# Building a graph's adjacency matrices: laps without a branch, crowded groups done afterwards, one weight product for three

## The chip, the cores and the metric

The kernel runs on one core of one Trainium2 chip. The metric is device time in microseconds for one execution, the median of three runs. The profile is of one further execution.

## The reference, cut to what matters

Four graph layers run one after the other over 3125 nodes and 103125 edges (a GCN with edge weights, a GAT with four heads, a dot-product attention, a two-step GraphSAGE), each followed by a layer norm. All four need sums over the edges that arrive at each node:

```python
msgs = edge_val[:, None] * xw[edge_col]
out = segment_sum(msgs, edge_row, num_segments=3125)      # layer 0
out = segment_sum(h[src] * alpha[:, :, None], dst, 3125)   # layer 1, softmax over each node's edges
numer = segment_sum(w[:, None] * V[sender], receiver, 3125)   # layer 2, softmax again
agg = segment_sum(x[src], dst, 3125) / max(deg, 1)         # layer 3, twice
```

The edges come sorted by destination (`dst`), on average 33 to a node.

## The kernel before, in words

Instead of gathering and scattering, the kernel builds two dense matrices in device memory (`adjacency`): for each pair (destination, source) how many edges there are and the sum of their weights. Afterwards every layer is dense matrix work over tiles of 128 nodes.

The change lies in the first two of its stages.

`edge_tables` prepares the edges. Nodes are taken in groups of three destinations (`WD = 3`), 1056 groups in all. VectorE finds by comparisons where each group's edges start in the sorted list (`start`, and `held`, which is `start` limited so that 128 entries can be read). GpSimd then fetches, for each group, the 128 edges from that place on (`own`, nine indirect DMAs, 128 groups each). TensorE transposes them in three batches (L388), ScalarE copies the transposes out of PSUM (`ids`, `weight`, L416), and VectorE unpacks each batch (the helper at L263 to L283) into the table `near`: for edge slot p of group w, a key (destination in the group times 40, plus the high part of the source), a low part of the source (0 to 79), and the weight as three bf16 parts. Groups that hold more than 128 edges need further chunks. For them the stage also makes flat tables in one partition, `before_row` (running count of extra chunks) and `first_row`, and a table `limits` that holds, in all partitions, up to which edge each group has been read. Each flat row takes nine transposes (L374) and a copy (L408), one row after the other; `limits` takes one more row, a product with a row of ones (L379), and a copy (L411). TensorE issues all of these ahead of the transposes at L388, and ScalarE ahead of the copies at L416.

`build_matrices` runs 88 laps of twelve groups. In each lap

- VectorE makes one-hot rows of the low parts (L483) and of the keys (L485), and multiplies the former by each of the three weight parts (L489, three instructions);
- TensorE multiplies keys by low parts, three matmuls for each group, 36 in a lap (L525), of which the last stands alone behind the part described next;
- ScalarE copies the 120 x 1920 results from PSUM to one of two halves of `bm_stage` (L557), after the store of that half two laps earlier has landed;
- SyncE stores the half, 900 KB (L566).

The one-hots, the four PSUM banks that a lap writes and the staging area are double: lap n uses what lap n - 2 used. VectorE and TensorE both call `beyond` in each lap: they read two entries of `before_row` into registers (L451), compare them (L456), and only if they differ go through the lap's groups with further chunks. The loop holds two laps to a round (L446). The stage ends when the last store has landed; the next stage reads what was stored.

Of the kernel before, what the change touches and what calls it, by code (L numbers as in the profile page):

```python
# [56 lines left out]
RING = 2  # L57
DST_BITS = 12
# [48 lines left out]
def edge_tables(nc, k):  # L107

    with ExitStack() as ctx:
# [3 lines left out]
        def sem(name):  # L113
# [14 lines left out]
        edge_i = sb("edge_i", [P, ECOL], I32)  # L128
# [23 lines left out]
        lim = sb("lim", [P, WT])  # L152
# [4 lines left out]
        row = sb("flat_row", [1, NWP])  # L157
# [6 lines left out]
         flat_taken, spread) = map(  # L164
            sem, ("consts", "pads", "noughts", "below_ready", "falls_ready", "counted", "rows_ready", "pair_ready",
                  "starts_ready", "cols_turned", "cols_taken", "et_turned", "et_taken", "dve_done", "start_ready",
                  "shifted", "more_ready", "et_summed", "before_ready", "flattened", "flat_taken", "et_spread"))
# [4 lines left out]
        N_CONSTS = 17  # L172
# [35 lines left out]
        def _(pool):  # L208
# [23 lines left out]
            pool.iota(edge_i[:, :], pattern=[[P, ECOL]], base=0, channel_multiplier=1).then_inc(consts, 1)  # L232
# [19 lines left out]
        def _(dve):  # L252
# [50 lines left out]
            step(dve.tensor_copy(k.edge_at[:], edge_i[:]))  # L303
# [18 lines left out]
            step(dve.tensor_scalar(lim[:], held[:], float(P), None, ALU.add))  # L322
            floor(first[:], lim[:], P)
# [3 lines left out]
            step(dve.tensor_tensor(more[:], end[:], lim[:], ALU.is_gt))  # L327
            step(dve.tensor_tensor(more[:], more[:], past[:], ALU.mult))
# [63 lines left out]
        def _(act):  # L392
# [13 lines left out]
            for n, flat_row in enumerate((k.before, k.first, row)):  # L406
# [3 lines left out]
            act.wait_ge(spread, 1)  # L410
            act.activation(k.lim[:].rearrange("p (b c) -> p b c", c=BW), ps[:, 2:2 + BATCHES, 0:BW], ACT.Copy)  # L411
# [7 lines left out]
def build_matrices(nc, k):  # L419


    with ExitStack() as ctx:
# [3 lines left out]
        def sem(name):  # L426
            return ctx.enter_context(nc.semaphore(name))

        OH = sb("bm_oh", [P, RING, LW // 2, 1 + PARTS, SL, 2], BF16)
        gate = sb("bm_gate", [P, 1])  # L430
        more_key = sb("bm_more_key", [P, P], BF16)
        more_oh = sb("bm_more_oh", [P, 1 + PARTS, SL], BF16)
        stage = sb("bm_stage", [KEYS, 2, LW, 2, SL])
        ps = ctx.enter_context(nc.psum_tensor("bm_ps", [P, 8, BANK], F32))
        used, lows, made, copied, more_step, more_made, more_used = map(
            sem, ("bm_used", "bm_lows", "bm_made", "bm_copied", "bm_more_step", "bm_more_made", "bm_more_used"))
# [5 lines left out]
        WIDE = 2 * SL  # L442

        def each_lap(eng, work):
# [8 lines left out]
        def beyond(eng, lap, work):  # L453

            most = LAPS * LW * NCH
            with eng.If(table(eng, k.before, lap * LW, most) < table(eng, k.before, lap * LW + LW, most)):  # L456
                with eng.Fori(0, BANKS) as b:
                    with eng.Fori(0, PER_BANK) as i:
                        w = eng.snap(lap * LW + b * PER_BANK + i)
                        begin = table(eng, k.before, w, most)  # L460
                        end = table(eng, k.before, w + 1, most)
                        first = table(eng, k.first, w, NCH)
                        with eng.If(begin < end):
                            with eng.Fori(begin, end) as at:
                                c = nc.s_assert_within(eng.snap((at - begin) + first), 0, ECOL - 1,
                                                       skip_runtime_bounds_check_because=WHY)
                                work(at, w, c, b, i)
                        table(eng, k.first, w, NCH)
                table(eng, k.first, lap * LW, NCH)

        @block.vector
        def _(dve):
            dve.sem_inc(more_used, 1)

            def onehots(lap, u, two):
                wide_low, wide_key = [P, LW // 2, SL, 2], [P, LW // 2, KEYS, 2]

                def spread(f, wide):
                    return (k.near[:, f, bass.ds(lap * LW, LW)].rearrange("p (a b) -> p a b", b=2).unsqueeze(2)
                            .to_broadcast(wide))  # L480

                dve.wait_ge(used, lap + 1)
                dve.tensor_tensor(OH[:, u, :, 0], k.low_grid[:].unsqueeze(1).to_broadcast(wide_low),  # L483
                                  spread(1, wide_low), ALU.is_equal).then_inc(lows, 1)
                dve.tensor_tensor(k.KEY[:, u, :, 0:KEYS], k.key_grid[:].unsqueeze(1).to_broadcast(wide_key),  # L485
                                  spread(0, wide_key), ALU.is_equal)
# [5 lines left out]
                def more(at, w, c, b, i):  # L492
                    dve.wait_ge(more_used, at + 1)
                    dve.tensor_tensor(gate[:], k.edge_at[:, bass.ds(c, 1)], k.lim[:, bass.ds(w, 1)], ALU.is_ge
                                      ).then_inc(more_step, 1)
                    dve.tensor_scalar(more_key[:], k.iota_key[:], k.key_base[:, bass.ds(w, 1)],
                                      k.col_key[:, bass.ds(c, 1)], ALU.add, ALU.is_equal).then_inc(more_step, 1)
                    dve.tensor_scalar(more_oh[:, 0], k.iota_low[:], k.col_low[:, bass.ds(c, 1)], None, ALU.is_equal
                                      ).then_inc(more_step, 1)
                    dve.wait_ge(more_step, at * 3 + 3)  # L500
                    dve.tensor_scalar(more_key[:], more_key[:], gate[:], None, ALU.mult)
                    for v in range(PARTS):
                        last = dve.tensor_scalar(more_oh[:, 1 + v], more_oh[:, 0], k.col_parts[:, v, bass.ds(c, 1)], None,
                                                 ALU.mult)
                    last.then_inc(more_made, 1)

                beyond(dve, lap, more)

            each_lap(dve, onehots)

        @block.tensor
        def _(pe):
# [3 lines left out]
            def products(lap, u, two):  # L516
                def place(i, v):
                    b, c = divmod(i, PER_BANK)
                    return ps[:, 4 * u + b, c * WIDE + SL * (v > 0):(c + 1) * WIDE]

                def body(i, planes):
# [1467 lines left out]
```

## Time and profile before

| | |
|---|---|
| time, median of 3 runs | 2430.63 us (2427.82 to 2435.46) |
| the profiled execution | 2439.62 us, of which its span 2437.9 us |
| edge tables | 0 to about 81 us |
| the 88 laps | about 81 to 443 us, the last store to about 450 us |
| busy over the whole span | PE 78%, VectorE 72%, ScalarE 46%, GpSimd 5% |

Engines are PE (TensorE's matmuls), PEld (its weight loads), DVE (VectorE), ACT (ScalarE), POOL (GpSimd) and SP (SyncE). A row of the timeline gives start, duration, engine, line, operation, what it writes and reads, its shapes and, in brackets, how long the engine was idle before it and what ended the idleness; "x35" are 35 instructions merged into a row. A q behind an engine's name is its sequencer: register loads, comparisons and branches, which do not count as busy. The shares over the whole span say little here, since the change touches only the first 450 us; all rows below are therefore of stretches in it, but for those on instruction fetches.

### The profile page before, as it was taken

To read this page: it belongs to the slowest core of one execution; us is meant where nothing else is said; L and a number is where in the kernel's file an instruction comes from. 1 tells how busy PE (TensorE), PEld (TensorE's weight loads), DVE (VectorE), ACT (ScalarE), POOL (GpSimd) and SP (SyncE) were. 2 spreads that over 40 slices of the span, in tenths; PEclk is the share of its full clock that TensorE was granted. 3 is DMA by queue.
4 is the path that set the end of the run, shared out by engine and by line. 5 is a ranking of instruction groups with operands and counts; after the bars stand their busy time and mean duration, and the time that the engine had idled before them with its cause. 6 is when DMAs were issued, how large, how long until landed. Compare 5 with 4: busy or idle time off the path is not lost. (4 is left out here: it accounts for less than half of the span.)

```text
span 2437.9 us, 44362 instructions
## 1 busy us (share of the span) xinstructions
PE 1902.0 (78%) x16121; PEld 1441.9 (59%) x16122; DVE 1753.2 (72%) x1874; ACT 1133.4 (46%) x1959; POOL 127.3 (5%) x225
## 2 busy tenths in 40 slices
PE   3456666699478888898888888873899999498794
PEld 2456555444456666676666667652688887354452
DVE  4887877100359999999999999855788885572375
ACT  1344444100257777677777777632666664101001
POOL 4000000000000000000000000000000000010120
PEclk6787877799689999999999999986899999699897
DMA  3488888999023443322444432211865650492492
GB/s 103 116 235 230 231 221 220 237 270 244 6 62 103 111 110 109 97 50 73 110 109 110 109 79 59 82 39 35 162 129 108 133 108 3 188 409 112 204 420 76
DMA packets 582353, 341.98 MB, mean 140 GB/s; under 512 B 397008, under 2 KB 574312, under 8 KB 575640
## 3 DMA queue, kind: packets, MB, share of 16 engines
q1 hardware_dynamic: 579928, 338.61, 50.4%
q0 software_dynamic: 720, 1.77, 0.3%
q10 hardware_dynamic: 1648, 0.83, 0.1%
q8 instruction: 37, 0.61, 0.1%
q14 instruction: 20, 0.16, 0.0%
HBM read 214.18 MB, written 127.01 MB: 140 GB/s over the span
## 5 line engine op out<-in xcount | busy, mean ns | idle before, releaser
L1207 ACT ACTIVATE exponentials<-gr_ps,att_cols 128x256 f32<-128x256 f32 (+1 forms) x1300 | 493.3, 491 | 185.1 <-PE gr_ps L1097 183.3
L1097 PE MATMUL gr_ps<-ident,gr_r 128*128 128x128 f32 x2500 | 381.8, 292 | 69.0 <-DVE gr_r L1315 67.0
L1097 PEld LDWEIGHTS gr_ps<-ident,gr_r 128*128 128x128 f32 x2500 | 284.1, 147 | 153.0 <-issue 130.8
L1128 PE MATMUL gr_ps<-exponentials,heads 128*33 128x128 f32 x5000 | 363.5, 277 | 14.1 <-DVE exponentials L1322 14.1
L1322 DVE SCALAR_TENSOR_TENSOR exponentials<-exponentials,gr_count_t 128x3072 f32<-128x3072 f32 (+1 forms) x104 | 349.0, 3355 | 21.9 <-ACT exponentials L1207 17.9
L1288 DVE CUSTOM_DVE_ANT_0 gr_unread<-gr_src_rows,gr_closed 128x3125 bf16<-128x3125 f32 (+1 forms) x100 | 344.2, 3442 | 17.0 <-ACT gr_closed L1200 16.6
L525 PE MATMUL bm_ps<-bm_oh,key_onehots 128*128 128x80 bf16 (+1 forms) x3168 | 228.9, 238 | 146.6 <-issue 119.4
L525 PEld LDWEIGHTS bm_ps<-bm_oh,key_onehots 128*128 128x128 bf16 x3168 | 202.7, 112 | 172.8 <-issue 169.3
L1128 PEld LDWEIGHTS gr_ps<-exponentials,heads 128*33 128x33 f32 x5000 | 254.1, 110 | 80.5 <-issue 55.9
L557 ACT ACTIVATE bm_stage<-bm_ps 120x1920 f32<-120x1920 f32 x88 | 156.0, 1773 | 220.8 <-DMA adjacency<-bm_stage 119.5
L798 PE MATMUL sage_ps<-sage_counts,sage_parts 128*128 128x400 bf16 x1200 | 207.4, 337 | 14.6 <-DVE sage_counts L832 14.6
L1315 DVE TENSOR_SCALAR gr_r<-gr_src_rows,gr_lift_u,gr_floor_u 128x3125 f32<-128x3125 f32 (+1 forms) x100 | 188.0, 1921 | 13.1 <-PE gr_ps L1097 7.5
L798 PEld LDWEIGHTS sage_ps<-sage_counts,sage_parts 128*128 128x128 bf16 x1200 | 118.6, 99 | 104.1 <-DVE sage_counts L832 16.0
L1546 PE MATMUL ar_ps<-KT,ar_left 128*128 128x400 f32 x400 | 147.1, 512 | 16.2 <-DVE ar_low_u L1637 14.7
L489 DVE TENSOR_TENSOR bm_oh<-bm_oh,near 128x960 bf16<-128x960 bf16 x264 | 157.4, 652 | 0.0
L698 PE MATMUL agg_gcn_ps<-agg_gcn_ring,agg_gcn_left 128*128 128x400 f32 x400 | 142.5, 512 | 14.3 <-DMA agg_gcn_ring<-adjacency 14.2
L1565 PEld LDWEIGHTS ar_ps<-ar_pt,X 128*128 128x128 f32 x1250 | 145.5, 192 | 11.5 <-ACT ar_pt L1609 4.5
L1565 PE MATMUL ar_ps<-ar_pt,X 128*128 128x128 f32 x1250 | 147.8, 275 | 0.0
L832 DVE CAST sage_counts<-sage_ring 128x3200 bf16<-128x3200 f32 x50 | 93.7, 1874 | 47.6 <-POOL sage_ring L788 47.6
L710 DVE COPY agg<-agg_gcn_ps 128x1600 f32<-128x1600 f32 x1 | 1.8, 1825 | 173.4 <-PE agg_gcn_ps L698 173.4
L698 PEld LDWEIGHTS agg_gcn_ps<-agg_gcn_ring,agg_gcn_left 128*128 128x128 f32 x400 | 75.6, 193 | 81.3 <-issue 30.6
L1609 ACT ACTIVATE ar_pt<-ar_ps 128x512 f32<-128x512 f32 (+1 forms) x175 | 84.0, 547 | 77.4 <-PE ar_ps L1555 77.4
(319 smaller groups left out, 1970.2 us busy)
## 6 DMA issues: line engine op xcount, KB each, us to landing
sage_ring<-count_by_source SPq DMA_DIRECT2D x50, 1600.0 KB, 9.3
adjacency<-bm_stage SPq DMA_DIRECT2D x88, 900.0 KB, 5.8
agg_gcn_ring<-adjacency SPq DMA_DIRECT2D x25, 1600.0 KB, 14.4
gr_count<-adjacency SPq DMA_DIRECT2D x25, 1600.0 KB, 9.3
ar_counts<-adjacency SPq DMA_DIRECT2D x25, 1600.0 KB, 9.1
count_by_source<-gr_count_t SPq DMA_DIRECT2D x12, 3200.0 KB, 16.7
fg_node<-gat_node_sums SPq DMA_DIRECT2D x1, 1650.0 KB, 6.3
count_by_source<-gr_count_t SPq DMA_DIRECT2D x1, 1600.0 KB, 7.1
```

What stands on the lines that cost most here:

```text
L489: last = dve.tensor_tensor(OH[:, u, :, 1 + v], OH[:, u, :, 0], spread(2 + v, wide_low), ALU.mult)
L525: last = pe.matmul(place(i, v), k.KEY[:, u, a, :, b], moving, start=i % PER_BANK == 0 and v == 0, stop=True, skip_group_check=True)
L557: act.activation(stage[:, u].rearrange("p (b w) v c -> p b (w v c)", b=BANKS), ps[0:KEYS, BANKS * u:BANKS * (u + 1), 0:PER_BANK * WIDE], A ...
L698: last = pe.matmul(ps[:, b, 0:CW], left[:, u, :], ring[:, u, b * CW:(b + 1) * CW], start=False, stop=True, skip_group_check=True)
L798: last = pe.matmul(ps[:, b, 0:CW], parts[:, u, i, :], counts[:, u, b * CW:(b + 1) * CW], start=False, stop=True, skip_group_check=True)
L1097: last = pe.transpose(ps[:, i % RINGS, c:c + P], r[:, j, s * P:(s + 1) * P], k.ident[:])
L1128: last = pe.matmul(ps[j * PAIR:j * PAIR + C + 1, 7, 0:P], heads[:, h, s, :], e[:, s, j * P:(j + 1) * P], start=s == 0, stop=s == NT - 1, s ...
L1207: last = act.activation(e[:, s, 0:w], ps[:, i % RINGS, c:c + w], ACT.Exp, bias=cols[:, h, s:s + 1])
L1288: dve.tensor_tensor_reduce(out=unread[:, 0:n], in0=src_rows[:, h, 0:n], in1=closed[:, j, 0:n], scale=1.0, scalar=FLOOR, op0=ALU.subtract, ...
L1315: last = dve.tensor_scalar(r[:, j, 0:n], src_rows[:, h, 0:n], lift_u[:, h, j:j + 1], floor_u[:, h, j:j + 1], ALU.add, ALU.max)
L1322: dve.scalar_tensor_tensor(part, part, 1.0, count_t[:, first:last, 0:w], ALU.min, ALU.mult).then_inc(weighed, 1)
L1565: last = pe.matmul(ps[:, 7, 0:P], k.X[:, first + j, :], pt[:, i, j * P:(j + 1) * P], start=first + j == 0, stop=first + j == NT - 1, skip_ ...
```

## The change

- **Laps.** `beyond` is gone from the laps: neither VectorE nor TensorE reads a table or branches inside one. The 36 matmuls of a lap stand together.
- **Crowded groups.** Behind the last lap, `each_crowded` goes down from all groups to 96, to twelve, to one, wherever the running count differs, and rebuilds a group of more than 128 edges whole: VectorE makes one-hots for each chunk, TensorE accumulates, ScalarE copies out and stores over the group's place. ScalarE begins this only once all stores of the laps have landed.
- **Tables.** `first` now counts from the group's own start, and a group counts as crowded by `end - start > 128`. `limits`, `edge_at` and the flat row that fed `limits` are gone, with nine transposes, six matmul instructions and two ScalarE copies.
- **Products.** The weights' one-hots of a lap come from one VectorE instruction over 2880 elements in each partition, where there were three over 960. For that the parts are the outer dimension of `bm_oh`, and `near` is laid out lap by lap, so the unpacking writes runs of twelve elements.
- **Loop.** Four laps make a round instead of two.

```diff
+UNROLL = 4
 # edge_tables
-            step(dve.tensor_copy(k.edge_at[:], edge_i[:]))
-            step(dve.tensor_scalar(lim[:], held[:], float(P), None, ALU.add))
-            floor(first[:], lim[:], P)
+            floor(first[:], start[:], P)
+            step(dve.tensor_tensor(crowd[:], end[:], start[:], ALU.subtract))
-            step(dve.tensor_tensor(more[:], end[:], lim[:], ALU.is_gt))
-            step(dve.tensor_tensor(more[:], more[:], past[:], ALU.mult))
+            step(dve.scalar_tensor_tensor(more[:], crowd[:], float(P), past[:], ALU.is_gt, ALU.mult))
-                unpack(ids[:, cols], weight[:, cols], BW, k.near[:, 0, cols], k.near[:, 1, cols],
-                       [k.near[:, 2 + v, cols] for v in range(PARTS)], k.key_base[:, cols])
+                mine = [k.near[:, b * (BW // LW):(b + 1) * (BW // LW), f, :] for f in range(2 + PARTS)]
+                unpack(ids[:, cols], weight[:, cols], BW, mine[0], mine[1], mine[2:], k.key_base[:, cols])
-            for n, column in enumerate((before, first, lim)):
+            for n, column in enumerate((before, first)):
-            pe.wait_ge(flat_taken, 3)
-            for b in range(BATCHES):
-                last = pe.matmul(ps[:, 2 + b, 0:BW], ones[0:1, :], row[:, b * BW:(b + 1) * BW], start=True, stop=True)
-            last.then_inc(spread, 1)
-            for n, flat_row in enumerate((k.before, k.first, row)):
+            for n, flat_row in enumerate((k.before, k.first)):
-            act.wait_ge(spread, 1)
-            act.activation(k.lim[:].rearrange("p (b c) -> p b c", c=BW), ps[:, 2:2 + BATCHES, 0:BW], ACT.Copy)
 # build_matrices
-            with eng.Fori(0, LAPS // 2) as two:
-                for u in range(2):
-                    work(two * 2 + u, u, two)
+            with eng.Fori(0, LAPS // UNROLL) as some:
+                for u in range(UNROLL):
+                    work(some * UNROLL + u, u % 2, some * (UNROLL // 2) + u // 2)
+        def each_crowded(eng, work):
+            def inside(w, sizes):
+                begin = table(eng, k.before, w, MOST)
+                end = table(eng, k.before, w + sizes[0], MOST)
+                with eng.If(begin < end):
+                    if len(sizes) == 1:
+                        work(w, begin, end)
+                    else:
+                        with eng.Fori(0, sizes[0] // sizes[1]) as i:
+                            inside(eng.snap(i * sizes[1] + w), sizes[1:])
+                    table(eng, k.first, w, NCH)
+            inside(0, (LAPS * LW, 96, LW, 1))
 # VectorE, one lap
-                for v in range(PARTS):
-                    last = dve.tensor_tensor(OH[:, u, :, 1 + v], OH[:, u, :, 0], spread(2 + v, wide_low), ALU.mult)
-                last.then_inc(made, 1)
-                beyond(dve, lap, more)
+                low = OH[:, u, 0].rearrange("p a c b -> p (a c b)").unsqueeze(1)
+                dve.tensor_tensor(OH[:, u, 1:].rearrange("p v a c b -> p (v a) c b"), low.to_broadcast([P, PARTS, LW * SL]),
+                                  near(2, PARTS).to_broadcast([P, PARTS * (LW // 2), SL, 2]), ALU.mult).then_inc(made, 1)
 # TensorE, one lap
-                for i in range(LW - 1):
-                    body(i, range(PARTS))
-                body(LW - 1, range(PARTS - 1))
-                beyond(pe, lap, more)
-                body(LW - 1, range(PARTS - 1, PARTS)).then_inc(used, 1)
+                for i in range(LW):
+                    a, b = divmod(i, 2)
+                    for v in range(PARTS):
+                        moving = OH[:, u, 0:2, a, :, b] if v == 0 else OH[:, u, 1 + v, a, :, b]
+                        last = pe.matmul(place(i, v), k.KEY[:, u, a, :, b], moving, start=i % PER_BANK == 0 and v == 0,
+                                         stop=True, skip_group_check=True)
+                last.then_inc(used, 1)
             each_lap(pe, products)
+            pe.wait_ge(copied, LAPS + 2)
+            each_crowded(pe, redo)
 # ScalarE
             each_lap(act, copy_out)
+            for s in range(2):
+                act.wait_ge(stored[s], 16 * (LAPS // 2) + 16)
+            each_crowded(act, redo)
```

## Rows read from the trace of the kernel before

**Rows 1.** Busy time of each engine over the laps, with granted clock, DMA share, GB/s.
```profile
82.00:443.00 361.00, 228.88 (x3168) 202.73 (x3168) 279.02 (x439) 155.98 (x88) 0.00 (x0) 0.81 0.81 221
```

**Rows 2.** Waits in the laps: total us, times, longest us.
```profile
ACT bm_stage L557 <- DMA adjacency<-bm_stage: 119.5, 54, 3.2
ACT bm_stage L557 <- PE bm_ps L525: 101.3, 34, 22.4
```

**Rows 3.** The timeline of ScalarE's copies, one to a lap.
```profile
88.54 1.77 ACT L557 ACTIVATE bm_stage<-bm_ps 120x1920 f32<-120x1920 f32 x1 [22.37 <-PE bm_ps L525]
96.51 1.77 ACT L557 ACTIVATE bm_stage<-bm_ps 120x1920 f32<-120x1920 f32 x1 [3.11 <-DMA adjacency<-bm_stage]
...
239.19 1.77 ACT L557 ACTIVATE bm_stage<-bm_ps 120x1920 f32<-120x1920 f32 x1 [1.90 <-DMA adjacency<-bm_stage]
...
246.56 1.77 ACT L557 ACTIVATE bm_stage<-bm_ps 120x1920 f32<-120x1920 f32 x1 [1.53 <-DMA adjacency<-bm_stage]
...
389.05 1.77 ACT L557 ACTIVATE bm_stage<-bm_ps 120x1920 f32<-120x1920 f32 x1 [2.93 <-DMA adjacency<-bm_stage]
...
441.15 1.77 ACT L557 ACTIVATE bm_stage<-bm_ps 120x1920 f32<-120x1920 f32 x1 [1.03 <-PE bm_ps L525]
```

**Rows 4.** The stores of the laps (L566), from issue to landing.
```profile
DMA to landing us min/median/max: 5.4/5.8/7.0
```

**Rows 5.** Instructions of TensorE and VectorE in the laps, by line.
```profile
L525 PE MATMUL bm_ps<-bm_oh,key_onehots 128*128 128x80 bf16 (+1 forms) x3168 | 228.9, 238 | 146.6 <-issue 119.4 <-DVE bm_oh L489 26.5
...
L489 DVE TENSOR_TENSOR bm_oh<-bm_oh,near 128x960 bf16<-128x960 bf16 x264 | 157.4, 652 | 0.0
...
L485 DVE TENSOR_TENSOR key_onehots<-key_grid,near 128x1440 bf16<-128x1440 int16 x88 | 79.3, 902 | 0.0
L483 DVE TENSOR_TENSOR bm_oh<-low_grid,near 128x960 bf16<-128x960 int16 x87 | 57.3, 658 | 75.7 <-PE bm_ps L525 74.0 <-issue 1.4
```

**Rows 6.** The timeline of TensorE: 35 matmuls of a lap, at either clock.
```profile
243.01 1.88 PE L525 MATMUL bm_ps<-bm_oh,key_onehots 128*128 128x160 bf16 x35 [0.39 <-issue]
...
433.73 3.29 PE L525 MATMUL bm_ps<-bm_oh,key_onehots 128*128 128x160 bf16 x35 [0.40 <-issue]
```

**Rows 7.** Table reads and branch (lines L451, L456): ns min/median/max.
```profile
L451 PEldq TENSOR_LOAD <-before_row x176: 298/624/1487, 86.2 to 440.0; - x176
...
L456 PEldq COMPARE_BRANCH  x88: 212/212/253, 87.9 to 440.6; - x88
```

**Rows 8.** The timeline from the last load of edges to the end of unpacking.
```profile
45.44 0.95 POOL L244 DMA_INDIRECT own<-edge_pairs,held_i  x1 [0.30 <-issue]
...
52.45 1.12 ACT L408 ACTIVATE first_row<-ps_tab 1x1152 int32<-1x1152 f32 x1 [2.17 <-PE ps_tab L374]
53.62 1.58 PEld L374 LDWEIGHTS ps_tab<-ident,lim 128*1 128x1 f32 x9 [1.71 <-ACT first_row L408]
...
61.04 1.56 PE L388 MATMUL ps_tab<-ident,own 128*128 128x128 f32 x6
...
63.16 0.36 DVE L271 TENSOR_SCALAR scratch_i<-ids 128x384 int32<-128x384 int32 x1 [16.22 <-ACT weight L416]
...
79.75 0.56 DVE L283 TENSOR_TENSOR near<-scratch,near 128x384 bf16<-128x384 f32 x1
```

**Rows 9.** DMA issues up to 100 us: the indirect loads of edges, us to landing.
```profile
own<-edge_pairs,held_i POOLq DMA_INDIRECT x9, 2.8
```

**Rows 10.** The timeline of VectorE: one unpaired product at two sizes.
```profile
28.16 1.09 DVE L281 TENSOR_TENSOR scratch<-col_weight,col_parts_b 128x896 f32<-128x896 f32 x1
...
67.31 0.56 DVE L281 TENSOR_TENSOR scratch<-weight,near 128x384 f32<-128x384 f32 x1
```

**Rows 11.** One round of the GAT stage's loop (L1020): busy time, instruction counts.
```profile
924.50:996.10 71.60, 61.82 (x664) 49.01 (x660) 70.32 (x41) 51.60 (x115) 3.35 (x2) 0.98 0.34 93
```

**Rows 12.** DMA queues over the whole span: packets, MB, share of 16 engines.
```profile
q8 instruction: 37, 0.61, 0.1%
```

**Rows 13.** DMA queues from 1000 to 1500 us; it is the only queue listed.
```profile
q1 hardware_dynamic: 98448, 46.82, 34.5%
```

More of the change, by code:

```diff
@@ L442, in build_matrices @@
         WIDE = 2 * SL
+        MOST = LAPS * LW * NCH
         def each_lap(eng, work):
-            with eng.Fori(0, LAPS // 2) as two:
-                for u in range(2):
-                    work(two * 2 + u, u, two)
+            with eng.Fori(0, LAPS // UNROLL) as some:
+                for u in range(UNROLL):
+                    work(some * UNROLL + u, u % 2, some * (UNROLL // 2) + u // 2)
         def table(eng, t, w, most):
             return eng.value_load(t[0:1, bass.ds(w, 1)], min_val=0, max_val=most)
[L453 to L469, printed above, removed]
@@ L471, in _, with onehots, near @@
         @block.vector
         def _(dve):
-            dve.sem_inc(more_used, 1)
-            def onehots(lap, u, two):
+            dve.sem_inc(redo_used, 1)
+            def onehots(lap, u, nth):
                 wide_low, wide_key = [P, LW // 2, SL, 2], [P, LW // 2, KEYS, 2]
-                def spread(f, wide):
-                    return (k.near[:, f, bass.ds(lap * LW, LW)].rearrange("p (a b) -> p a b", b=2).unsqueeze(2)
-                            .to_broadcast(wide))
+                def near(first, fields):
+                    mine = k.near[:, bass.ds(lap, 1), first:first + fields]
+                    return mine.rearrange("p l f (a b) -> p (l f a) b", b=2).unsqueeze(2)
@@ L487, in onehots @@
                 dve.wait_ge(lows, lap + 1)
-                for v in range(PARTS):
-                    last = dve.tensor_tensor(OH[:, u, :, 1 + v], OH[:, u, :, 0], spread(2 + v, wide_low), ALU.mult)
-                last.then_inc(made, 1)
[L492 to L501, printed above, removed]
+                low = OH[:, u, 0].rearrange("p a c b -> p (a c b)").unsqueeze(1)
@@ L502, in more @@
                     for v in range(PARTS):
-                        last = dve.tensor_scalar(more_oh[:, 1 + v], more_oh[:, 0], k.col_parts[:, v, bass.ds(c, 1)], None,
+                        last = dve.tensor_scalar(redo_oh[:, 1 + v], redo_oh[:, 0], k.col_parts[:, v, bass.ds(c, 1)], None,
                                                  ALU.mult)
-                    last.then_inc(more_made, 1)
-                beyond(dve, lap, more)
+                    last.then_inc(redo_made, 1)
+                with dve.Fori(begin, end) as at:
+                    chunk(at)
@@ L514, in _, with products @@
             pe.sem_inc(copied, 2)
-            def products(lap, u, two):
+            def products(lap, u, nth):
                 def place(i, v):
                     b, c = divmod(i, PER_BANK)
-                    return ps[:, 4 * u + b, c * WIDE + SL * (v > 0):(c + 1) * WIDE]
-                def body(i, planes):
+                    return ps[:, BANKS * u + b, c * WIDE + SL * (v > 0):(c + 1) * WIDE]
+                pe.wait_ge(copied, lap + 1)
+                pe.wait_ge(made, lap + 1)
+                for i in range(LW):
@@ L529, in products @@
-                pe.wait_ge(copied, lap + 1)
-                pe.wait_ge(made, lap + 1)
-                for i in range(LW - 1):
-                    body(i, range(PARTS))
-                body(LW - 1, range(PARTS - 1))
-                def more(at, w, c, b, i):
-                    pe.wait_ge(more_made, at + 1)
-                    for v in range(PARTS):
-                        out = ps[:, bass.ds(b + 4 * u, 1), bass.ds(i * WIDE + SL * (v > 0), WIDE - SL * (v > 0))]
-                        out = out.rearrange("p b c -> p (b c)")
-                        last = pe.matmul(out, more_key[:], more_oh[:, 0:2] if v == 0 else more_oh[:, 1 + v],
-                                         start=False, stop=True, skip_group_check=True)
-                    last.then_inc(more_used, 1)
@@ L544, in products, with redo, chunk @@
-                beyond(pe, lap, more)
-                body(LW - 1, range(PARTS - 1, PARTS)).then_inc(used, 1)
+                last.then_inc(used, 1)
+            def redo(w, begin, end):
+                def chunk(at, start):
+                    pe.wait_ge(redo_made, at + 1)
+                    for v in range(PARTS):
+                        last = pe.matmul(ps[:, 0, SL * (v > 0):WIDE], redo_key[:], redo_oh[:, 0:2] if v == 0 else redo_oh[:, 1 + v],
+                                         start=start and v == 0, stop=True, skip_group_check=True)
+                    last.then_inc(redo_used, 1)
+                pe.wait_ge(redo_copied, begin + 1)
+                chunk(begin, True)
+                with pe.Fori(begin + 1, end) as at:
+                    chunk(at, False)
@@ L1921, in program @@
             k.own_in = [ctx.enter_context(nc.semaphore(f"own_in{b}")) for b in range(BATCHES)]
-            k.near = esb("near", [P, 2 + PARTS, NWP], BF16)
+            k.near = esb("near", [P, NWP // LW, 2 + PARTS, LW], BF16)
             k.before = esb("before_row", [1, NWP], I32)
             k.first = esb("first_row", [1, NWP], I32)
-            k.lim = esb("limits", [P, NWP])
-            k.edge_at = esb("edge_at", [P, ECOL])
             k.col_key = esb("col_key", [P, ECOL])
```

65 lines of the change are left out of this document (43 added, 22 removed).

## The prediction

> **What bounds the kernel now.** The change touches two stages, so I read them by themselves. First the busy times over the laps [rows 1]: in 361 us DVE is busy 279, PE 229, ACT 156, the DMA engines 81%. Nothing is full, so something circular sets the pace. Next ScalarE's waits, since its copy is where a lap meets its store [rows 2]: 54 of 88 copies are released by the landing of the store two laps back, 34 by TensorE. Two mechanisms take turns. The timeline of the copies [rows 3] gives the pace: from the first to the last 441.15 - 88.54 = 352.6 us, 87 intervals, 4.05 us a lap.
>
> The store's circle: copy 1.77 us, issue and hand-over some 0.2, store landing 5.8 [rows 4], sum 7.8 us for two laps. The 54 copies that a landing released, first at 96.51 and last at 389.05, start on average 7.81 us behind the copy two laps earlier (3.90 a lap); one of the shortest is 239.19 to 246.56, 7.37 us [rows 3]. I also sorted them by how evenly the two halves alternate: 28 of them, whose previous interval was 3.4 to 4.3 us, average 7.66; 8 with a shorter one average 8.28, since two stores then overlap more; 17 with a longer one 7.81.
>
> TensorE's circle: PE idles 146.6 us in the laps, 119.4 of it put down to issue, and the first one-hot of a lap waits 74.0 us for TensorE [rows 5]. The issue time is the two table reads and the branch in front of the last matmul: 0.62 us median for a read, up to 1.49, and 0.21 for the branch [rows 7], and the last matmul is what frees the one-hots and releases the copy. At the low level (granted clock 0.5, or 1.2 GHz; the mean over the laps is 0.81) 35 matmuls take 3.29 us, at the high one 1.88 [rows 6]. With reads and last matmul a slow lap comes near 4.9 us, above the store's 3.9; a fast one stays below.
>
> In front of the laps a chain is exposed: DVE stands idle 16.22 us until the first transposed edges are there at 63.16 [rows 8], then unpacks without a gap to 80.3.
>
> **Part by part. Tables.** TensorE now turns to the edges' transposes (L388) once `first_row` is copied at 52.45 + 1.12 = 53.57, or even before, since the edges lie in other PSUM banks and it waits only for the loads: the transposes start at the end of `first`'s own, near 52.4. The loads are no later: nine indirect ones, each landing 2.8 us after issue [rows 9], the last issued from 45.44 to 46.4 [rows 8], so landed near 49.2. ScalarE takes `ids` after 53.57, not 62.2. Gone are the nine transposes at 53.62, one copy, six matmuls of a broadcast and another copy, to 61.04 [rows 8]. Everything from L388 on moves by 61.04 - 52.4 = 8.6 us. One small VectorE step of the chain goes too (0.2). The casts into `near` now write runs of twelve; a cast of this size takes as long as the 0.36 us instruction at 63.16 [rows 8], and at worst the 0.56 of a product of the same size [rows 10]. Two casts in each of three batches: 0 to 1.2 us, taken 0.6. Were the transposes' move not to pay, it would be for late loads, and these have 3 us in hand even against the first batch. Term: -8.6 - 0.2 + 0.6 = **-8.2 us**. The copy of `edge_at` and one iota lie beside waits for transposes and DMAs and count nothing.
>
> **Laps, TensorE.** 36 matmuls together: about 3.4 us at the low level, 1.95 at the high one, and up to 0.4 between laps [rows 6], so 3.8 and 2.4. Both lie under the store's pace, the first barely.
>
> **Laps, VectorE.** From 960 elements in 0.652 to 1440 in 0.902 us [rows 5] an element costs 0.52 ns, so 2880 cost 0.652 + 1920 x 0.52 = 1.65 us for 3 x 0.652 = 1.96. The five durations sum to 3.52, yet DVE is busy 279.0 / 88 = 3.17 a lap, so each of four seams overlaps by 0.09. New: 0.66 + 0.90 + 1.65 - 0.17 = 3.04 us. The gain of 0.13 is hidden, and worth nothing while stores set the pace. A buffer's round through both engines is 3.04 + 3.4 + 0.3 = 6.8 us at the low level, under 7.7.
>
> **Laps, the store.** Copies, stores and the two halves stay as they are, so this circle is what is left. Its price is bounded by 7.37 and 8.28 us for two laps. Without TensorE's late laps the halves should alternate more evenly, though not perfectly, as the overlap corrects short intervals only slowly; I take 7.7, that is 3.85 a lap, near the 7.66 of the even ones. 87 x 3.85 = 335.0 for 352.6: **-17.7 us**. Bounds: 87 x 3.69 gives -32, 87 x 4.05 gives 0. DMA share would rise to 0.81 x 4.05 / 3.85 = 0.85, still not full.
>
> **Behind the laps.** ScalarE waits for the last store and only then reads two entries and branches; the stage's end waits for it. What is exposed is two reads, a branch and the register work between. TensorE's rows give 2 x 0.30 + 0.21 for a quiet memory [rows 7] and I add as much again for register work: 1.8 us; with the longest reads 2 x 1.49 + 0.21 and the same register work, 4.2. Taken **+1.8 us**. The same reads on TensorE and VectorE lie under the last copy and the last store. No group is crowded in this data: all 439 DVE instructions of the laps are five to a lap and all 3168 matmuls 36 to a lap [rows 1], so nothing is rebuilt.
>
> **The unroll.** Half the loop branches go; each is far below the hand-over of 0.4 and hidden. But the body grows to 4 x 36 x 2 = 288 matmul and load instructions on TensorE. In the trace, a loop round of the GAT stage holds 664 + 660 of them [rows 11], and between 1000 and 1500 us, over several rounds of it, no instruction queue moves a packet [rows 13]. So a body of 288 should not be fetched again: 0 us. The Trainium skill (Runtime: NRT & Kernel Launch, Instruction fetch mechanics) says that a taken branch whose target is outside a window of two 16 KiB pages, 512 instructions, must fetch it by DMA first; by that rule a body that straddles three pages would pay in each of 22 rounds. The same section gives TensorE a store of 2048 instructions, and by this trace's 1324 in a round the larger figure fits.
>
> **Sum.** -8.2 - 17.7 + 1.8 = -24.1 us. The profiled execution took 2439.6 (span 2437.9), so it would take 2415.5. It lies 9.0 above the median shown, 2430.6; against that the forecast is 2406.5 us.
>
> **The rivals.** What a measurement can tell from no change is about 0.3%, 7.3 us.
>
> 1. Stores spread: with every lap bound by them they land later, and the pace stays at 4.05. For it: pairs close together already average 8.28. Against: 28 even ones at 7.66, a DMA share of only 0.81. Then only -8.2 + 1.8 = -6.4 is left: 2424, which is within the bound. Chance 0.08.
> 2. Stores evenly spaced and fast, 3.69 a lap: -32 - 8.2 + 1.8 = -38: 2392. Chance 0.09.
> 3. Slower, by VectorE: the product over 2880 elements, with the low parts repeated by an outer step of zero, loses its rate of two elements. The unpaired rate is (1.09 - 0.56) / 512 = 1.04 ns [rows 10], so 1.09 + 1984 x 1.04 = 3.15 us, and a VectorE lap is 0.66 + 0.90 + 3.15 - 0.17 = 4.54, with a hand-over of 0.1 4.64. It decides as soon as this exceeds 3.85. 87 x (4.64 - 4.05) = +51, sum +45: 2475. Against: the three products of before already read a repeated operand at 0.52 ns an element, all types are the same, and only which operand has the zero step outside is new. Chance 0.04.
> 4. Slower, by fetches: each of 22 rounds fetches two blocks of TensorE's code. The span's 37 packets took 0.1% of 16 engines' time [rows 12], 39 us or 1.05 each, so 2.1 a round, 46 us if nothing hides them, sum at worst +22: 2453. It decides from the point where four laps' slack against the store, 0.05 each at the low level and 1.4 at the high one, is used up; over the mixture most would hide. Chance 0.03 for a slower kernel.
>
> My forecast has 0.72, and 0.04 is left for what I don't see. Within it, 3.78 to 3.95 a lap and the tail's bounds give 2398 to 2416. The range takes in rival 1 and most of what lies towards rival 2: 2394 to 2424. Faster by over 0.3%: 0.85 (forecast, rival 2, and most of the rest); within (rival 1): 0.08; slower: 0.07.
>
> **What would show it.** Right: the idle time of DVE before the first unpacking falls from 16.2 to about 7.6 us and unpacking ends near 72; L489's group is one instruction a lap of 1.65 us; PE's idle time put down to issue in the laps shrinks to hand-overs, and nearly all copies at L557 wait for a landing; copies start 3.85 us apart, 335 us from first to last; between the last landing and the next stage some 1.8 us of ScalarE's reads. Wrong: landings clearly above 5.8; a product of over 3 us; instruction packets all through the laps; or copies still released by TensorE at the low level, where 3.8 against 3.85 is the closest margin of all.

## The result, and the profile after

The changed kernel takes 2445.59 us (median of 4 runs, 2444.22 to 2448.16) beside 2431.48 for the kernel before (here also of 4): ratio 1.0059, 95% interval 1.0041 to 1.0077. It is slower by 14 us where 24 us less were forecast, and outside the range. The profiled execution took 2444.22 us, its span 2442.5; that of the kernel before was 2437.9. The two traces differ by only 4.6 us, since the profiled execution of before (2439.62) was 8 us slower than its median.

The busy times over the laps come first, then ScalarE's waits (total us, times, longest us):

```profile
72.00:440.00 368.00, 216.61 (x3168) 203.50 (x3168) 265.92 (x264) 153.05 (x87) 0.00 (x0) 0.80 0.84 214
```

```profile
ACT bm_stage L550 <- DMA adjacency<-bm_stage: 203.4, 83, 3.7
PEld bm_ps L519 <- ACT bm_stage L550: 158.7, 83, 3.3
PE bm_ps L519 <- ACT bm_stage L550: 145.9, 83, 3.1
```

The mechanism changed as forecast. VectorE has three instructions a lap (264 for 439), no idle time of the matmuls is put down to issue any more [rows 5], and nearly all copies wait for a store's landing, 83 of the 87 in this stretch, for 54 of 88 [rows 2]. TensorE waits for the copies. Yet the circle that is left is slower than the mixture it replaced. The timeline of the copies and the stores' landings:

```profile
78.12 1.77 ACT L550 ACTIVATE bm_stage<-bm_ps 120x1920 f32<-120x1920 f32 x1 [22.27 <-PE bm_ps L519]
...
439.28 1.77 ACT L550 ACTIVATE bm_stage<-bm_ps 120x1920 f32<-120x1920 f32 x1 [2.61 <-DMA adjacency<-bm_stage]
443.49 1.77 ACT L550 ACTIVATE bm_stage<-bm_ps 120x1920 f32<-120x1920 f32 x1 [2.44 <-DMA adjacency<-bm_stage]
```

```profile
DMA to landing us min/median/max: 5.8/6.3/7.9
```

From first to last copy 365.4 us, for 352.6 before [rows 3]: 4.20 us a lap. The shortest, the median and the longest landing are all later than before, by 0.4, 0.5 and 0.9 us [rows 4]. The other parts are near their forecasts. The product, from the groups of VectorE, takes what was worked out:

```profile
L477 DVE TENSOR_TENSOR bm_oh<-bm_oh,near 128x2880 bf16<-128x2880 bf16 x88 | 145.4, 1653 | 0.0
```

In the timeline of the tables, the edges' transposes stand at 51.20 and the first unpacking at 53.34, behind 7.41 us of idleness for 16.22 [rows 8]; a cast into the new layout takes 0.36, no more than before:

```profile
51.20 1.48 PE L380 MATMUL ps_tab<-ident,own 128*128 128x128 f32 x6
...
53.34 0.36 DVE L269 TENSOR_SCALAR scratch_i<-ids 128x384 int32<-128x384 int32 x1 [7.41 <-ACT weight L406]
...
57.09 0.36 DVE L278 CAST near<-weight 128x384 bf16<-128x384 f32 x1
...
69.92 0.56 DVE L281 TENSOR_TENSOR near<-scratch,near 128x384 bf16<-128x384 f32 x1
```

The last unpacking starts 9.8 us earlier than before, the first copy 10.4. Behind the laps ScalarE's two reads stand between the last landing and the next stage (ns min/median/max, first and last start), here with the next stage's first matmuls:

```profile
L442 ACTq TENSOR_LOAD <-before_row x2: 282/380/477, 451.3 to 452.1; - x2
```

```profile
453.50 2.83 PE L751 MATMUL agg_gcn_ps<-zeros 128*128 128x400 bf16 x8 [14.86 <-PEq L412]
```

So the loss is one term: 87 laps at 4.20 us and not 3.85. Nothing in the diff touches a copy or a store of the laps. What it does touch is where the staging area lies: what was deleted ahead of it in on-chip memory moves `bm_stage` from address 105728, a multiple of 128, to 97504, which is 96 above one. The suspicion to test was that the stores read more slowly from there.

Of these 8224 bytes in each partition, the shapes in the kernel account for 8192 by the tables `limits` (1152 floats) and `edge_at` (896 floats). That is 64 x 128, so the tables alone would have left the area at a multiple of 128. The other 32 are the place of `bm_gate`, a tile of one float, which stood just ahead of the area and went with `beyond`.

### The profile page after: what moved, and what is told of

It reads as the page before. It is cut to its first block and busy times, and to the rows that moved or that the text cites. A ratio compares the mean times of both kernels' runs of the same rounds, so it can differ in the third digit from the quotient of the medians.

```text
span 2442.5 us, 42242 instructions
## 1 busy us (share of the span) xinstructions
PE 1883.7 (77%) x16106; PEld 1439.1 (59%) x16107; DVE 1740.0 (71%) x1696; ACT 1134.6 (46%) x1958; POOL 120.1 (5%) x224
## 3 DMA queue, kind: packets, MB, share of 16 engines
q0 software_dynamic: 720, 1.77, 0.3%
## 5 line engine op out<-in xcount | busy, mean ns | idle before, releaser
L1138 PE MATMUL gr_ps<-exponentials,heads 128*33 128x128 f32 x5000 | 363.5, 277 | 14.1 <-DVE exponentials L1332 14.1
L519 PE MATMUL bm_ps<-bm_oh,key_onehots 128*128 128x80 bf16 (+1 forms) x3168 | 216.6, 240 | 166.7 <-ACT bm_stage L550 145.9
L477 DVE TENSOR_TENSOR bm_oh<-bm_oh,near 128x2880 bf16<-128x2880 bf16 x88 | 145.4, 1653 | 0.0
L471 DVE TENSOR_TENSOR bm_oh<-low_grid,near 128x960 bf16<-128x960 int16 x88 | 57.9, 658 | 98.0 <-PE bm_ps L519 97.0
```

Of the source, the lines that this page charges most:

```text
L519: last = pe.matmul(place(i, v), k.KEY[:, u, a, :, b], moving, start=i % PER_BANK == 0 and v == 0, stop=True, skip_group_check=True)
L1138: last = pe.matmul(ps[j * PAIR:j * PAIR + C + 1, 7, 0:P], heads[:, h, s, :], e[:, s, j * P:(j + 1) * P], start=s == 0, stop=s == NT - 1, s ...
```

## The experiments

The address of the staging area stands beside each kernel, as its distance above a multiple of 128. "Before" had a median of 2434.99, 2433.31 and 2434.66 us on the three occasions (kernels 1 to 4, 5 to 8, 9 to 12). Packet time is an estimate worked out from the DMA share and GB/s of a stretch: share x 16 engines x 640 bytes / rate. The share is rounded to 0.01, which leaves some 0.2 ns either way.

**1. The changed kernel with the staging area at 0** (8 floats of padding), the base from here on.

```diff
+        sb("bm_pad", [P, 8])
         stage = sb("bm_stage", [KEYS, 2, LW, 2, SL])
```

> The changed kernel with 32 unused bytes ahead of the staging area, which moves it from address 97504 (96 above a multiple of 128) to 97536 (a multiple of 128), as it was in the kernel before (105728). Nothing else differs. Theory A, the address: the stores read 640-byte packets from a place in on-chip memory where packets take longer, 40.3 ns on average for 37.4. Then packets fall back to about 37.4 ns, the landing from 6.3 to about 5.8 us, the copies' pace from 4.20 to about 3.85 us a lap, and the time by 87 x 0.35 = 30 us, to about 2415 (2408 to 2422). Theory B, the rhythm: landings are longer because every lap now waits for its store, so that two stores always overlap, and the address does not matter. Then landing 6.3, 4.2 a lap and 2445 stay.

Measured: 2417.23 us, ratio 0.9921 (0.9892 to 0.9949). Its copies, their waits for a landing, the landings, and the stretch from 100 to 340 us, then the same stretch of the changed kernel and of the kernel before:

```profile
78.94 1.78 ACT L551 ACTIVATE bm_stage<-bm_ps 120x1920 f32<-120x1920 f32 x1 [21.42 <-PE bm_ps L520]
...
418.69 1.77 ACT L551 ACTIVATE bm_stage<-bm_ps 120x1920 f32<-120x1920 f32 x1 [2.20 <-DMA adjacency<-bm_stage]
```

```profile
ACT bm_stage L551 <- DMA adjacency<-bm_stage: 183.3, 85, 4.0
```

```profile
DMA to landing us min/median/max: 5.4/5.8/7.6
```

```profile
100.00:340.00 240.00, 137.16 (x2219) 128.44 (x2220) 186.99 (x186) 108.15 (x62) 0.00 (x0) 0.88 0.86 236
```

```profile
100.00:340.00 240.00, 139.85 (x2057) 131.24 (x2058) 175.67 (x174) 101.88 (x58) 0.00 (x0) 0.81 0.87 220
```

```profile
100.00:340.00 240.00, 150.47 (x2168) 132.96 (x2169) 191.43 (x302) 107.20 (x61) 0.00 (x0) 0.84 0.85 233
```

Thirty-two unused bytes are worth 28 us between the two medians, or 32 if each is set against the kernel before on its own occasion (-17.8 and +14.1). The DMA engines of the changed kernel are as busy as the base's (0.87 and 0.86) and move less (220 and 236 GB/s): 40.5 ns a packet for 37.3. Before it was 37.4. The pace is 339.75 / 87 = 3.91 us a lap. Every lap still waits for its store here (85 of 88 copies), so the rhythm does not lengthen the landing; theory B is out.

**2. The kernel before with the staging area at 96** (24 floats of padding in each partition).

> The kernel before with 96 unused bytes ahead of the staging area, so that it lies 96 above a multiple of 128, as in the changed kernel. Theory A: landing about 6.3 us for 5.8. The 54 laps that were bound by the store go from 3.90 to about 4.2 us and some of the other 34, bound by TensorE near 4.3 to 4.9, become bound by the store too: about 4.3 us a lap over all, +22 us, 2453 (2445 to 2462). Theory B: the same as before, within 4 us.

Measured: 2455.7 us, ratio 1.0081 (1.0055 to 1.0108), landings and the same stretch:

```profile
DMA to landing us min/median/max: 5.8/6.2/7.7
```

```profile
100.00:340.00 240.00, 148.59 (x2034) 131.83 (x2035) 179.40 (x282) 100.36 (x57) 0.00 (x0) 0.80 0.86 217
```

The address alone makes the old kernel 20.7 us slower. With the address equal the changed kernel is faster at 0, 2417.2 against 2435.0. At 96 it is 2445.6 against 2455.7, but these are from different occasions, and the intervals of their ratios (1.0041 to 1.0077, 1.0055 to 1.0108) overlap, so a gain at 96 is not shown.

**3 and 4. The changed kernel at 32 and at 64** (16 and 24 floats of padding).

> The changed kernel with 64 unused bytes: the staging area 32 above a multiple of 128. Theory A1, reads go in aligned pieces, and cost rises with the distance of a packet's start from an aligned address below: packets start alternately 32 and 160 above a multiple of 256, for 0 and 128 in the first run and 96 and 224 in the changed kernel; a third of the way between these two: packets 38.4 ns, about 2425. The Trainium skill (DMA: Bandwidth & Descriptors, How a descriptor splits into AXI transactions) has such a rule: 23 beats of 32 bytes on average here, for 22 at a multiple of 128 and 25 at 96. Theory A2, only a 64-byte grid matters: as slow as the changed kernel, 2445. Theory B: 2445.

> The changed kernel with 96 unused bytes: the staging area 64 above a multiple of 128. Theory A1: packets start at 64 and 192 above a multiple of 256, two thirds of the way: 39.4 ns, about 2435. By the page's rule 24 beats on average. Theory A2, a 64-byte grid: as fast as the first run, about 2415. Theory B: 2445.

Measured: 2440.2 us (ratio 1.0016, 0.9999 to 1.0034) at 32 and 2429.26 (0.9973, 0.9956 to 0.9991) at 64. First the two rows of 32, then those of 64:

```profile
DMA to landing us min/median/max: 5.8/6.3/8.8
```

```profile
100.00:340.00 240.00, 139.16 (x2072) 130.37 (x2073) 174.07 (x173) 102.43 (x58) 0.00 (x0) 0.81 0.84 221
```

```profile
DMA to landing us min/median/max: 5.7/6.0/7.8
```

```profile
100.00:340.00 240.00, 141.05 (x2127) 131.85 (x2125) 179.39 (x179) 105.58 (x60) 0.00 (x0) 0.82 0.87 228
```

| above a multiple of 128 | packet ns | landing us, median | time us | ratio |
|---|---|---|---|---|
| 0 | 37.3 | 5.8 | 2417.2 | 0.9921 |
| 64 | 39.1 | 6.0 | 2429.3 | 0.9973 |
| 32 | 38.9 | 6.3 | 2440.2 | 1.0016 |
| 96 | 40.5 | 6.3 | 2445.6 | 1.0059 |

Neither form of the theory fits both columns. Packet time is least at 0, alike at 32 and 64, and longest at 96, close to A1. The landing, which sets the pace, follows a 64-byte grid first (0 and 64 against 32 and 96), as A2 has it, but within the grid 0 still beats 64. The Trainium skill (DMA: Bandwidth & Descriptors, How a descriptor splits into AXI transactions) says that a read of a packet begins at the 256-byte boundary below its start, and that the unused bytes still cost beats of 32 bytes. Worked out from that rule as an estimate, the packets here cost 22, 23, 24 and 25 beats on average at 0, 32, 64 and 96; the measured packet times go that way but for a tie in the middle, the landings don't.

**5. Three products again, at 0.** The fused instruction became a loop of three over `OH[:, u, 1 + v]`.

> The changed kernel with the staging area at a multiple of 128 (the base of all four kernels here) and the lap's weight products as three instructions over 960 elements again. Theory A (address, and laps bound by the store): VectorE is busy 3.17 us a lap instead of 3.05, both under the pace of 3.9, so nothing moves: 2417 (2413 to 2421), pace 3.90. Rival: the single product is what brought the laps' gain; then the pace goes back towards 4.05 and the time towards 2430.

Measured: 2417.41 us, ratio 0.9928 (0.99 to 0.9955), pace 3.90. As theory A had it: the single product gives nothing that can be measured while the store sets the pace.

**6. Table reads and branch back in the laps, at 0.**

```diff
+        def look(eng, lap):
+            begin = table(eng, k.before, lap * LW, MOST)
+            end = table(eng, k.before, lap * LW + LW, MOST)
+            with eng.If(begin < end):
+                table(eng, k.first, lap * LW, NCH)
...
+                look(dve, lap)
...
+                        if i == LW - 1 and v == PARTS - 1:
+                            look(pe, lap)
```

> The base with two table reads and a branch put back into each lap, on TensorE ahead of the last matmul and on VectorE at the lap's end; the branch is never taken. Theory A: TensorE's laps at the low clock pass the store's pace again, some 30 copies are released by TensorE, pace about 4.05, +13 us: 2430 (2424 to 2434). Rival: the reads cost nothing and the gain of the laps came from the rest (unroll, one product): 2417.

Measured: 2426.35 us, ratio 0.9968 (0.9951 to 0.9986), 9.1 above the base.

```profile
ACT bm_stage L560 <- DMA adjacency<-bm_stage: 162.5, 76, 3.4
ACT bm_stage L560 <- PE bm_ps L529: 46.4, 12, 22.4
```

The reads cost something, less than forecast. The runs scatter from 2420.66 to 2432.16, all above those of kernels 5 and 8 on the same occasion (2413.58 to 2420.4). The profiled one is the fastest of them, with a pace of 3.92 us, so the trace doesn't show where the 9 us of the median lie.

**7. Four staging areas, at 0.**

```diff
-        stage = sb("bm_stage", [KEYS, 2, LW, 2, SL])
+        stage = sb("bm_stage", [KEYS, 4, LW, 2, SL])
-        stored = [sem(f"bm_stored{s}") for s in range(2)]
+        stored = [sem(f"bm_stored{s}") for s in range(4)]
...
-                    work(some * UNROLL + u, u % 2, some * (UNROLL // 2) + u // 2)
+                    work(some * UNROLL + u, u % 2, (u, some))
...
-                act.wait_ge(stored[u], nth * 16 + 16)
-                act.activation(stage[:, u].rearrange(
+                q, some = nth
+                act.wait_ge(stored[q], some * 16 + 16)
+                act.activation(stage[:, q].rearrange(
...
```

The store uses `stage[:, q]` and `stored[q]` in the same way, and the waits behind the laps are for all four.

> The base with four staging areas instead of two, so that a copy waits for the store four laps back. If the circle of copy and store (7.8 us for two laps) is what bounds the laps, it opens, and the next bounds are TensorE at the low clock with its hand-over (3.6 to 3.8 us), VectorE (3.1) and what the DMA engines can move: they are busy 0.86 at 3.9, so 3.36 us a lap when full. Then a pace of 3.5 to 3.7, -17 to -35 us against the base: 2382 to 2400. Rival: stores that overlap more slow each other, and the DMA engines stay at some 236 GB/s whatever is queued: 3.85 to 3.9, 2412 to 2417.

Measured: 2352.86 us, ratio 0.9667 (0.9635 to 0.9698), 64 us below the base. The stretch, the landings and the first waits:

```profile
100.00:340.00 240.00, 148.09 (x2772) 138.48 (x2772) 232.97 (x233) 135.09 (x77) 0.00 (x0) 1.00 1.00 292
```

```profile
DMA to landing us min/median/max: 6.1/10.3/10.5
```

```profile
ACT bm_stage L552 <- DMA adjacency<-bm_stage: 101.0, 72, 1.5
```

240 us hold 77 copies, 3.12 us each, where the base had 62. A single store takes 10.3 us from issue to landing; over a pace of 3.12 that is some three in flight, and its length no longer sets the pace: the DMA engines are full, at 292 GB/s. The pace is below the 3.5 us of the expectation, and below the 3.36 at which it had the DMA engines full, since that took a packet's 37.3 ns as fixed; here a packet takes 35.1.

**8. Slots of 768 bytes, two areas, at 0.** The area became `[KEYS, 2, LW, 192]`, of which the first 160 floats of each slot are used.

> The base with each 640-byte slot of the staging area 768 bytes from the next, so that every packet starts at a multiple of 256 and none at 128 above it. Theory A1 (reads in aligned pieces of 256 bytes): packets get shorter again, by as much as from 64 to 0 above a multiple of 128 (1.6 ns) or a little more: 35 to 36 ns, landing 5.6, pace 3.8: 2409 (2404 to 2413). The page named with the earlier runs counts 20 beats here for 22. Theory A2 (only a 64-byte grid matters): 37.3 ns and 2417 stay. A slower ScalarE copy (three runs of 160 instead of one of 480) would show in its own row.

Measured: 2417.52 us, ratio 0.9933 (0.9911 to 0.9955).

```profile
DMA to landing us min/median/max: 5.4/5.8/7.7
```

```profile
100.00:340.00 240.00, 138.36 (x2206) 129.32 (x2205) 186.44 (x186) 108.42 (x62) 0.00 (x0) 0.87 0.83 236
```

The packets did shorten, to 36.0 ns, and the landing and the time did not; ScalarE's copy still takes 1.77 us. So the packets' mean duration isn't the pace; it goes with it only in part.

**9. Four areas, slots of 768, and the last wait moved** behind ScalarE's two reads, into `redo`.

> Four staging areas, each slot of 640 bytes 768 bytes from the next, and ScalarE's wait for the last stores moved into the rebuilding of a crowded group, so that its two table reads run beside the last stores. With four areas the DMA engines are full (share 1.00, packets 35.0 ns, 3.16 us a lap), so the packets' time is the pace. Theory A1: packets shorten by the 1.4 ns that the wide slots gave with two areas, 4%, and the pace falls until VectorE's 3.05 to 3.1 us holds it: -5 us. The moved wait gives 0.5 to 1 us. Together 2347 (2342 to 2351). Rival: packets are already as short as they get once requests queue, then 2352.

Measured: 2352.84 us, ratio 0.9668 (0.9654 to 0.9681): nothing over kernel 7 in the median. In the profiles the pace is 3.13 in both, so the wide slots give nothing; the moved wait shows, as the next stage's first matmul starts 12.3 us behind the last copy here and 14.0 in kernel 7.

**10. Four areas with the reads back in the laps.** Kernel 7 with the edit of kernel 6.

> Four staging areas, with the two table reads and the branch back in each lap on TensorE and VectorE. With the store's circle open nothing hides them any more. A lap on TensorE at the high clock is 1.95 of matmuls, some 1.5 of exposed reads, 0.2 of the last matmul and 0.4 of hand-over, 4.0, less at times; copies are then released by TensorE. Theory A: pace 3.6 to 4.0, 2390 to 2425, that is the change's branch-free laps are worth 40 to 70 us here, where they were worth at most 13 under two areas. Rival: reads are hidden here too, 2353.

Measured: 2424.67 us, ratio 0.9961 (0.9944 to 0.9979).

```profile
ACT bm_stage L561 <- PE bm_ps L529: 210.6, 88, 22.4
```

```profile
100.00:340.00 240.00, 152.53 (x2184) 134.84 (x2181) 183.70 (x182) 107.04 (x61) 0.00 (x0) 0.84 0.84 231
```

All 88 copies are released by TensorE, 61 in 240 us, 3.93 each. In these 240 us nearly all idle time of the matmuls is put down to issue, which is the reads, and little to VectorE, which has reads of its own. At the high clock too a lap can be long, as in this one:

```profile
L529 PE MATMUL bm_ps<-bm_oh,key_onehots 128*128 128x80 bf16 (+1 forms) x2184 | 152.8, 234 | 87.1 <-issue 82.2 <-DVE bm_oh L484 3.6
```

```profile
250.76 1.78 ACT L561 ACTIVATE bm_stage<-bm_ps 120x1920 f32<-120x1920 f32 x1 [2.39 <-PE bm_ps L529]
...
251.11 1.88 PE L529 MATMUL bm_ps<-bm_oh,key_onehots 128*128 128x160 bf16 x35 [0.39 <-issue]
...
255.56 1.77 ACT L561 ACTIVATE bm_stage<-bm_ps 120x1920 f32<-120x1920 f32 x1 [3.03 <-PE bm_ps L529]
```

With four areas the reads cost 72 us, with two only 9.

**11. Four areas at 96.** Kernel 7 without the padding.

> Four staging areas at address 97504, 96 above a multiple of 128, where the changed kernel has its own. Theory A: with full DMA engines the packets' time is the pace. They were 8% longer at 96 than at 0 with two areas: 3.16 x 1.08 = 3.41 us a lap, +22 us, 2375 (2365 to 2385). Rival: address and packet time only matter to the latency of one store, which four areas hide: 2353.

Measured: 2354.51 us, ratio 0.9679 (0.9663 to 0.9695), 1.7 above kernel 7, within both intervals.

```profile
100.00:340.00 240.00, 147.93 (x2772) 138.24 (x2770) 232.56 (x231) 134.03 (x77) 0.00 (x0) 1.00 1.00 292
```

My theory failed and the rival held: with four areas the address costs nothing that can be measured, neither in the time nor in the packets, at 35.1 ns as in kernel 7.

**12. Two laps to a round, two areas at 0.** `UNROLL = 2`.

> The changed kernel with the staging area at a multiple of 128 and two laps to a round of the loop instead of four. The laps are bound by the store, so the 22 more branches lie in idle time: 2417 (2413 to 2421), pace 3.90. Rival: the unroll carries part of the gain, at 0.2 us for each of 22 branches up to +5 us.

Measured: 2421.5 us, ratio 0.9942 (0.9923 to 0.9961), its runs from 2415.41 to 2424.26, pace 3.93. That is 4 above the base, with overlapping intervals: between nothing and the rival's 5 us it doesn't decide.

## Why the prediction was wrong

**The step that failed** is the sentence "Copies, stores and the two halves stay as they are, so this circle is what is left". The instructions stayed; their operand moved. I read what was removed as work saved and not as memory given back, and so never asked where `bm_stage` would lie. Two laps of the circle cost 8.4 us at the new address, above even the upper bound of 8.28 that I drew from rows in which two stores overlapped. It is shown both ways: putting the area back takes 28 us from the changed kernel, and moving it puts 21 us on the old one. The forecast also cut its own bound short: 8.28 us for two laps is 4.14 a lap, or +8 us over 87, and the sum used 4.05, or 0. With 4.14 its upper end would have been a kernel 1 us slower.

**Rival 1** forecast the sign of what was seen, late landings, by the wrong cause. At address 0 the landings are at 5.8 us with 85 of 88 copies released by them.

**The rest of the sum**, read from the base (kernel 1) against the kernel before, where the address is equal:

- Tables: -8.2 forecast, -9.0 measured: in the base the unpacking starts at 54.16 for 63.16 and its last instruction at 70.75 for 79.75. The casts cost nothing of the 0.6 allowed for. The first copy starts at 78.94 for 88.54, 0.6 more, without the reads ahead of its last matmul. In the changed kernel's trace the copy of `first_row` starts 1.0 us earlier than before (51.44 for 52.45), in the base's only 0.2 (52.27), which is the one VectorE step; so the 0.8 between the two are not the edit's.

```profile
54.16 0.36 DVE L269 TENSOR_SCALAR scratch_i<-ids 128x384 int32<-128x384 int32 x1 [7.41 <-ACT weight L406]
...
70.75 0.56 DVE L281 TENSOR_TENSOR near<-scratch,near 128x384 bf16<-128x384 f32 x1
```

- Laps: -17.7 forecast, 339.75 for 352.61 us or -12.9 measured. The mechanism was right, and the pace mis-sized: 3.91 for 3.85. I priced it from the evenly spaced copies of before (7.66 us for two laps), since the halves should alternate more evenly without TensorE's late laps. They hardly do: sorted as in the prediction, 50 of the base's copies are even, at 7.66 as forecast, and 33 uneven, at 8.0, where before it was 28 and 25. So the laps settle at 7.8, the mean of all 54. By kernel 5 none of this gain is the product's, by the medians of kernel 6 some 9 us are the reads'.
- Behind the laps: +1.8 forecast. In the changed kernel ScalarE's reads, of 0.48 and 0.28 us, start at 451.3 and the next stage's first matmul at 453.50: 2.2 us for the reads, the register work and the change of stage. From the last copy's start to that matmul it is 10.0 us there, 9.65 in the base and 9.2 before (441.15 to 450.38), so +0.4 for the base. The two can differ because this distance also holds the landing of one store, and single landings vary by more (5.4 to 7.6 us).
- In all the base's span is 22.9 us shorter than that of before, for a forecast of 24.1. Its median is 17.8 shorter; the profiled execution of before was 5 us above the median that the base's is compared with, so about as much of the terms above is scatter of that one execution, most likely in the laps.

**The unroll and the fetches**: as argued from the GAT loop, the body of 288 is not fetched again; the DMA view of the changed kernel from 100 to 440 us lists a single packet of instructions. **The product** runs at the rate worked out (1.653 us for 1.65).

**Why so much removed work moved so little** is settled by kernels 1, 6, 7 and 10. Two circles had nearly the same length: copy and store, 3.91 us a lap, and TensorE with its table reads, 3.93. Kernel 6 has both, and takes 2426.4 us. Taking the reads out gives 2417.2 (-9), doubling the areas 2424.7 (-2, within the scatter of kernel 10's runs, 2414 to 2434), and both together 2352.9 (-73). The prediction named both circles, and took the second only as a nuisance at the low clock ("a fast one stays below"). In kernel 10's rows 35 matmuls take 1.88 us and the copy still starts 4.80 us behind the one before.

**What stays open**: why the landing follows the four addresses in the order 0, 64, 32, 96 while packet time ties at 32 and 64, and why shorter packets in kernel 8 brought no earlier landing. No run puts the one-float tile back alone; that it alone took the area off the multiple of 128 is read from the shapes. Open is also whether the unroll gives up to 4 us.

## What to carry to other kernels

- A deleted buffer moves those allocated after it, as here, and a tile of four bytes can do the harm that two large tables do not. Before costing an edit as "the transfers stay the same", compare the addresses of what they read; for a store that is waited for, one line of padding is the cheapest experiment there is.
- When removing a stall gains little, look for a second circle of the same length and open both in one kernel. Here the two were worth 9 us and next to nothing alone, and 73 together.
- A staging area that waits for its own store's landing is bound by latency: the DMA share of 0.86 looked nearly full, and two more areas still took a fifth off each lap.

## What the runs showed of the hardware that was not expected

- Reads of 640-byte packets by a store took 37.3 ns from an area at a multiple of 128 bytes and 40.5 from one 96 above it, and the store landed 0.5 us later (5.8, 6.3). With four areas, and some three stores in flight, the difference was gone (35.1 ns at both).
- The DMA engines at share 0.86 moved 236 GB/s, at 1.00 they moved 292, more than in proportion: 37.3 ns a packet fell to 35.1.
- TensorE's granted clock from 100 to 340 us was 0.80 to 0.88 in the kernels at 3.9 to 4.3 us a lap, and 1.00 in kernels 7, 9 and 11, at 3.13 to 3.14, so it stayed at 2.4 GHz there. In kernel 7 the idle time ahead of the matmuls was 102.7 us, or 1.2 a lap, for 140.4 or 1.6 in the base. First kernel 7, then the base:

```profile
L520 PE MATMUL bm_ps<-bm_oh,key_onehots 128*128 128x80 bf16 (+1 forms) x3114 | 166.4, 210 | 102.7 <-ACT bm_stage L552 76.0 <-DVE bm_oh L478 26.6
```

```profile
L520 PE MATMUL bm_ps<-bm_oh,key_onehots 128*128 128x80 bf16 (+1 forms) x3120 | 194.5, 228 | 140.4 <-ACT bm_stage L551 138.3 <-DVE bm_oh L478 2.1
```
